# Edge windows of a graph layer: ranges packed into one register each, loops of five tiles, sums on two other engines, x loaded alone

## The reference, cut to what matters

```python
xn = _layernorm(x)
hp = xn @ weight
agg = segment_sum(hp[src] * edge_weight[:, None], dst)      # relu'd later
x = x + relu(agg) + mix(xn)                                 # linear attention
```

## Time and profile before

| | |
|---|---|
| median of three runs | 1304.54 us (1303.4 to 1308.75) |
| the profiled execution's own time | 1310.6 us |
| its span from first to last instruction | 1309.1 us |
| mean granted TensorE clock | 0.929 |
| PE busy | 1117.8 us (85%) |
| DVE busy | 540.6 us (41%) |
| ACT, POOL busy | 347.6 and 83.4 us |
| the windows | from 53.4 to 183.5 us of the span |

### The profile page before, as it was taken

How to read it: one execution, slowest core, us unless ns; L and a number is a source line. 1 busy time by engine, 2 the same in 40 slices (tenths; PEclk the granted TensorE clock), 3 DMA queues, 4 the chain that set the end, 5 groups by cost and what they waited for, 6 DMA issues and landing times.

```text
span 1309.1 us, 19993 instructions
## 1 busy us (share of the span) xinstructions
PE 1117.8 (85%) x7185; PEld 757.1 (58%) x7186; DVE 540.6 (41%) x1434; ACT 347.6 (27%) x881; POOL 83.4 (6%) x130
## 2 busy tenths in 40 slices
PE   2766679988999863999998659998979998988896
PEld 1456564465877651555554347777557777565652
DVE  7565565343555431111111035444325544376430
ACT  1000012012555430222222125554115555011320
POOL 5100000000000032001000050000000000000000
PEclk9897789998999975999999969999989999998898
DMA  7500004010100046940199671000111000000000
GB/s 198 141 1 1 1 1 193 32 57 17 31 26 3 1 185 244 388 177 19 60 401 398 244 271 43 25 9 2 64 73 41 25 9 2 33 1 0 1 1 39
DMA packets 18415, 113.06 MB, mean 86 GB/s; under 512 B 4718, under 2 KB 6245, under 8 KB 14135
## 3 DMA queue, kind: packets, MB, share of 16 engines
q1 hardware_dynamic: 12718, 100.95, 20.3%
q0 software_dynamic: 5632, 11.23, 3.3%
HBM read 103.04 MB, written 9.11 MB: 86 GB/s over the span
## 4 chain that ended last, share of the span: by engine, by line
PE 74%; DVE 8%; DMA 7%; issue 4%; ACT 3%; DVEq 3%; POOL 1%; SPq 0%; POOLq 0%; ACTq 0%
PE psum L514 11%; PE psum L669 8%; PE psum L819 7%; PE psum L800 7%; PE psum L692 5%; PE psum L526 5%; PE psum L723 5%; PE psum L674 4%; PE psum L705 4%; PE psum L581 4%; PE psum L878 3%; PE psum L900 3%; DMA arena<-in_moe_b 2%; PE psum L502 1%; DVE arena L1183 1%
## 5 line engine op out<-in xcount | busy, mean ns | idle before, releaser
L514 PE MATMUL psum<-arena 128*125 128x512 f32 x320 | 142.2, 605 | 2.6 <-ACT arena L913 2.0
L581 PE MATMUL psum<-arena 125*128 x975 | 85.6, 260 | 44.5 <-DVE arena L1183 41.4
L971 ACT ACTIVATE arena<-arena,small 125x625 f32<-125x625 f32 x120 | 97.0, 809 | 90.5 <-DVE small L1312 90.5
L669 PE MATMUL psum<-arena 128*128 128x313 f32 (+1 forms) x384 | 112.2, 443 | 8.5 <-DMA arena<-in_att 7.2
L800 PE MATMUL psum<-arena 128*64 128x512 f32 x448 | 101.7, 607 | 7.4 <-DMA arena<-in_moeW 6.0
L514 PEld LDWEIGHTS psum<-arena 128*125 128x125 f32 x320 | 60.9, 192 | 80.7 <-issue 74.9
L581 PEld LDWEIGHTS psum<-arena 125*128 125x128 bf16 x975 | 74.2, 119 | 54.5 <-issue 52.2
L819 PE MATMUL psum<-arena 128*64 128x256 f32 x896 | 99.8, 381 | 3.7 <-DMA arena<-in_moe_b 3.7
L1029 ACT ACTIVATE arena<-psum,cols 128x64 f32<-128x64 f32 x224 | 47.3, 361 | 198.6 <-PE psum L806 198.6
L669 PEld LDWEIGHTS psum<-arena 128*128 128x128 f32 x384 | 72.2, 194 | 37.9 <-issue 9.7
L1183 DVE TENSOR_SCALAR arena<-arena 125x628 bf16<-125x628 f16 x195 | 66.9, 382 | 63.3 <-issue 28.0
(11 more groups left out here) (242 smaller groups left out, 1335.6 us busy)
## 6 DMA issues: line engine op xcount, KB each, us to landing
arena<-in_moeW SPq DMA_DIRECT2D x16, 4096.0 KB, 17.7
arena<-in_att SPq DMA_DIRECT2D x36, 256.0 KB, 2.8
arena<-in_l1W SPq DMA_DIRECT2D x2, 2048.0 KB, 15.7
rows<-in_rows SPq DMA_DIRECT2D x1, 2500.0 KB
token_rows<-arena POOLq DMA_DIRECT2D x19, 128.0 KB, 10.5
expert_rows<-arena POOLq DMA_DIRECT2D x17, 128.0 KB, 10.0
arena<-token_rows POOLq DMA_DIRECT2D x16, 128.0 KB, 8.3
arena<-in_gnnWo SPq DMA_DIRECT2D x2, 1024.0 KB, 6.2
```

What stands on the lines that cost most here:

```text
L514: mm = pe.matmul(bank(b, NP, D), srcT[:, k, c * NP:(c + 1) * NP], ring[n % 2][:, k, :], start=(k == 0), stop=(k == KC - 1))
L581: mm = pe.matmul(psum[:, o + c * P:o + (c + 1) * P], one_src[:, s, c * NP:c * NP + P], hot_dst[:, bass.ds(e * P, P)], start=False, stop=False,
L669: mm = pe.matmul(bank(b, P, width), aw[:, w, k, :], srcT[:, k, o:o + width], start=(k == 0), stop=(k == KC - 1))
L971: act.activation(Sx[u % 3][h], Sx[u % 3][h], ACT.Exp, bias=small[0:NP, 80 + n:81 + n], scale=-1.0, accum_out=small[0:NP, 120 + n:121 + n]) ...
```

## The change

A round does five tiles, and there are five `one_src` buffers. The first tile and the number of rounds are packed as `64 * first + rounds`, so PE spreads one value instead of three; PE and DVE load one register for each window, all twenty ahead of the first window, and unpack them in registers at each window; the rounds before a window are added up in a register. ACT copies the counts and also the three weight parts (125 x 480) to one of two SBUF buffers; POOL adds the three parts in two instructions. PE waits for ACT's copies instead of DVE's sum. The statistics of x are taken piece by piece as x lands, ahead of `bounds`; the destination one-hot is written behind the layer norm. x is loaded in five pieces, alone; `gnnW` is issued when x is there, `mixWq` and the rest when `gnnW` is there, and POOL's zero rows wait for `gnnW` too. PE waits for the ranges only behind `hp`.

```diff
-GT = 3
+GT = 5
+KG = -(-ET // GT)
...
+        def tile_range(eng, packed):
+            return (eng.snap(packed >> 6, min_val=0, max_val=ET - 1), eng.snap(packed & 63, min_val=1, max_val=KG))
...
-            sp.dma_start(xres[:], ins["x"]).then_inc(ld_x, 16)
+            for c in range(NC):
+                sp.dma_start(xres[:, c, :], ins["x"][:, c, :]).then_inc(ld_x[c], 16)
+            for c in range(NC):
+                sp.wait_ge(ld_x[c], 16)
             sp.dma_start(ring[0], ins["gnnW"]).then_inc(ld_ring[0], 16)
+            sp.wait_ge(ld_ring[0], 16)
             sp.dma_start(ring[1], ins["mixWq"]).then_inc(ld_ring[1], 16)
             sp.dma_start(cols[:], ins["cols"]).then_inc(ld_const, 16)
-            sp.wait_ge(ld_x, 16)
...
-            pool.wait_ge(ld_x, 16)
+            pool.wait_ge(ld_ring[0], 16)
...
-            pool.wait_ge(win_full, NW)
+            for w in range(NW):
+                pool.wait_ge(parts_out, w + 1)
+                n = min(DW, N - DW * w)
+                p3 = parts[w % 2].rearrange("p c (v d) -> p c v d", v=3)
+                pool.tensor_tensor(p3[:, :, 0, 0:n], p3[:, :, 0, 0:n], p3[:, :, 1, 0:n], ALU.add).then_inc(part_sum, 1)
+                pool.wait_ge(part_sum, w + 1)
+                pool.tensor_tensor(WT[:, :, DW * w:DW * w + n], p3[:, :, 0, 0:n], p3[:, :, 2, 0:n],
+                                   ALU.add).then_inc(wt_out, 1)
...
-            for v, spread in enumerate((ident, ident, upper)):
-                mm = pe.matmul(bank(5, 1, WMIN, WMIN * v), w_cols[:, min(v, 1):min(v, 1) + 1], spread[0:NW, 0:WMIN],
-                               start=True, stop=True)
-            mm.then_inc(range_rows, 1)
-            pe.wait_ge(range_ready, 1)
+            pe.matmul(bank(5, 1, WMIN), w_cols[:, 1:2], ident[0:NW, 0:WMIN],
+                      start=True, stop=True).then_inc(range_rows, 1)
...
+            pe.wait_ge(range_ready, 1)
+            ranges = [pe.value_load(bounds[0:1, w:w + 1], min_val=1, max_val=64 * ET + KG) for w in range(NW)]
+            before = 0
...
-            ahead = tile_range(0)
             for w in range(NW):
-                first, k, before = ahead
+                first, k = tile_range(pe, ranges[w])
                 o = window_banks(w)
                 if w >= 4:
-                    pe.wait_ge(wt_out, w - 3)
+                    pe.wait_ge(parts_out, w - 3)
...
-                if w + 1 < NW:
-                    ahead = tile_range(w + 1)
...
+                before = pe.snap(before + k, min_val=w + 1, max_val=(w + 1) * KG)
...
             product_cols("mq", T1, 1, window_out)
+            pe.wait_ge(cnt_out, NW)
...
+            pe.wait_ge(wt_out, NW)
...
+                sums = psum[0:NP, o:o + NC * P].rearrange("p (c x) -> p c x", x=P)
+                act.activation(cntT[:, :, DW * w:DW * w + n], sums[:, :, 3 * DW:3 * DW + n], ACT.Copy).then_inc(cnt_out, 1)
+                if w >= 2:
+                    act.wait_ge(wt_out, w - 1)
+                act.activation(parts[w % 2], sums[:, :, 0:3 * DW], ACT.Copy).then_inc(parts_out, 1)
...
-            ve.tensor_copy(w_cols[:, 1:2], n_i[:, 1:2]).then_inc(range_cols, 1)
+            ve.scalar_tensor_tensor(w_cols[:, 1:2], w_cols[:, 0:1], 64.0, n_i[:, 1:2], ALU.mult,
+                                    ALU.add).then_inc(range_cols, 1)
+            for c in range(NC):
+                ve.wait_ge(ld_x[c], 16)
+                i_ = chunk_stats(xres, c)
+            link(i_)
             ve.wait_ge(range_rows, 1)
-            ve.tensor_copy(bounds, bank(5, 1, 3 * WMIN).rearrange("p (v w) -> p v w", v=3)).then_inc(range_ready, 1)
-            ve.wait_ge(ld_x, 16)
-            layer_norm(0, xres, N1)
+            ve.tensor_copy(bounds, bank(5, 1, WMIN)).then_inc(range_ready, 1)
+            layer_norm(0, xres, N1, stats=False)
+            ve.tensor_tensor(hot_dst4[:, :, 3, :], low.unsqueeze(2).to_broadcast([NP, TP, DW]),
+                             iota_dst.unsqueeze(1).to_broadcast([NP, TP, DW]), ALU.is_equal).then_inc(dst_one, 1)
...
             ve.wait_ge(range_ready, 1)
-            ahead = tile_range(0)
+            ranges = [ve.value_load(bounds[0:1, w:w + 1], min_val=1, max_val=64 * ET + KG) for w in range(NW)]
+            before = 0
             for w in range(NW):
-                first, k, before = ahead
-                if w + 1 < NW:
-                    ahead = tile_range(w + 1)
+                first, k = tile_range(ve, ranges[w])
...
-                if w:
-                    window_sums(w - 1)
-            window_sums(NW - 1)
+                before = ve.snap(before + k, min_val=w + 1, max_val=(w + 1) * KG)
```

More of the change, by code:

```diff
@@ L32 @@
 NW = -(-N // DW)
-SW = N + GT
+SW = N + 3
 EX = 8
@@ L177, in build @@
         zero_bf = take(NP, P, dt=BF16)
-        zero_rows_sb = take(TT, D)
+        zero_rows_sb = at(o_D + TP * 2 * DW, TT, D)
         t_lo, t_hi = take(ET // 2, 2), take(ET // 2, 2)
@@ L182, in build @@
         w_end = take(NW, 8)
-        w_cols = take(NW, 3)
+        w_cols = take(NW, 2)
         n_i = take(NW, 2, dt=I32)
-        bounds = take(1, 3, WMIN, dt=I32)
+        bounds = take(1, WMIN, dt=I32)
+        parts = [at(o_T + 2 * KC * N + i * NC * 3 * DW, NP, NC, 3 * DW) for i in range(2)]
+        assert o_D + TP * 2 * DW + D <= AR
         assert oa[0] <= o_cnt
@@ L240, in build @@
         unit_full, freed_a, freed_v = sem("unit_full"), sem("freed_a"), sem("freed_v")
-        ld_edges, ld_x, ld_const = sem("ld_edges"), sem("ld_x"), sem("ld_const")
+        ld_edges, ld_const = sem("ld_edges"), sem("ld_const")
+        ld_x = [sem(f"ld_x{c}") for c in range(NC)]
         ld_ring = [sem(f"ld_ring{i}") for i in range(2)]
@@ L252, in build @@
         hot_ready, hot_free = sem("hot_ready"), sem("hot_free")
-        win_full, wt_out, cnt_out = sem("win_full"), sem("wt_out"), sem("cnt_out")
+        win_full, cnt_out = sem("win_full"), sem("cnt_out")
+        parts_out, part_sum, wt_out = sem("parts_out"), sem("part_sum"), sem("wt_out")
         fm_min, fm_exp = sem("fm_min"), sem("fm_exp")
@@ L588, in _ @@
                 mm.then_inc(win_full, 1)
+                before = pe.snap(before + k, min_val=w + 1, max_val=(w + 1) * KG)
             def window_out(unit):
                 w = NW - 4 + (unit % 8) // 2
-                pe.wait_ge(wt_out, w + 1)
+                pe.wait_ge(parts_out, w + 1)
             product_cols("mq", T1, 1, window_out)
+            pe.wait_ge(cnt_out, NW)
             for c in range(NC):
@@ L931, in _ @@
                 o, n = 512 * (2 * (w % 4)), min(DW, N - DW * w)
-                act.activation(cntT[:, :, DW * w:DW * w + n],
-                               psum[0:NP, o:o + NC * P].rearrange("p (c v d) -> p c v d", v=4, d=DW)[:, :, 3, 0:n],
-                               ACT.Copy).then_inc(cnt_out, 1)
+                sums = psum[0:NP, o:o + NC * P].rearrange("p (c x) -> p c x", x=P)
[3 more added lines that the diff above has]
+                act.activation(parts[w % 2], sums[:, :, 0:3 * DW], ACT.Copy).then_inc(parts_out, 1)
             def feature_exps(units):
@@ L1138, in _ @@
             i_.then_inc(range_in, 1)
-            ve.tensor_tensor(hot_dst4[:, :, 3, :], low.unsqueeze(2).to_broadcast([NP, TP, DW]),
-                             iota_dst.unsqueeze(1).to_broadcast([NP, TP, DW]), ALU.is_equal).then_inc(dst_one, 1)
             ve.wait_ge(range_turned, 1)
```

## The result

The changed kernel takes **1323.5 us** (median of four runs, 1321.4 to 1326.7) where the kernel before takes 1304.0: a ratio of 1.0144, 95% interval 1.0111 to 1.0177. It is slower by 19.5 us where 31 us less were forecast. The profiled execution took 1324.6 us with a span of 1323.0.

What follows compares the result with a forecast made beforehand. It took PE and DVE waiting on each other in rounds, and register loads at borders, as the bound. Rounds 81.4, borders 17.1 and clock 2.0 made 100.5 us for 130.2; with the front, 31 less: 1273.5 us, range 1259 to 1295.

Steps and rivals of the forecast that it cites:

- The rounds: Window loop: 46 rounds of five tiles at 1.77 us, set by PE's sequencer, 81.4 us.
- The borders without the sum: Between windows: register steps replace loads, 0.9 us a border, 17.1 us for 19; bounds 10 and 27.
- Front part: Before the windows: x at 12.5 us, `hp` ending at 40.4, first tile at 52.0 against 53.39.
- The clock: PE in the windows: a low start costs 2.0 us, then the high clock is taken as held.
- The sum: All windows: rounds, borders and clock start, 100.5 us instead of 130.2; with the front, 31 us less.
- POOL against DVE: Windows: POOL's sums hold up DVE's one-hots, 20 x 1.0 us on top, 1282 us; chance 0.17.
- the loads stick out whole: PE's twenty range loads, behind `hp`: no overlap with it, +8.3 us, 1282 us; chance 0.10.
- x alone: Front: x loaded alone is not early, at 18.6 us, moving all by 6, 1280 us; chance 0.06.
- slower: PE's matmuls in the windows: low clock throughout, 140 us against 130 before, 1302 to 1313 us; chance 0.05.

Runs made afterwards that it cites:

- reg_sum: The changed kernel with the rounds before a window held in one register on PE and DVE; 1269.7 us, 0.9727 of the kernel before.
- five_alone: The kernel before with only rounds of five tiles and five one-hot buffers; 1296.7 us, 0.9925 of the kernel before.

## Why the prediction was wrong

**The step that failed** is in the borders: I counted the running sum as one register step at a border, and costed three steps there with 0.36 to 1.26 us. The sum is made inside the rounds, once in each, out of all earlier windows: 564 steps more on each engine, 57.7 us of the windows, instead of 19 steps. I asked what a register step costs and not how many there are and where they stand. My price of a bare step was near enough (0.12 with its gap; measured 0.10). What I took for "a register" in the code was an expression; a value's bounds in the source say nothing of where it is computed. The diff alone did not say so, but a rival with its price should have stood there: everything that the change computes from a loop-carried value, worked out for the case that it is computed where it is used.

**The rest held, point by point.**
- *The rounds.* PE's sequencer as the bound at 1.77 us a round: 1.80 in the first window of the changed kernel, 1.80 and then 1.90 in reg_sum, whose sequencer goes from step to step through a whole round. That 1.77 came out so near is in part luck. The rounds of five_alone, which have the steps that I counted, take 1.66 in the first window; in reg_sum there is a step more in every round and another from the second window on, by all signs the unpacking, which I had put at the borders.
- *The borders without the sum.* Taken at 0.9, measured at some 0.3 in reg_sum, below my lower bound even: a term too dear by 11 us. It has no step of unpacking in it, only those of `reg_add` and of the loop's start. The unpacking stands in the rounds, and the longer rounds behind the first window (1.90) take back five of the 11.
- *Front part.* `hp` to end at 40.4, it was 40.6. x was not there at 12.5 but at 15.9, of which one us was waited for. Before, it came at 19.3; the 18.6 that I took for it is where DVE's wait began. PE's loads were to begin at 32.7 us and did. With 0.65 us for most of them and not 0.88 they ended at 46.6, so the first tile came at 48.2, between the two values I gave: 5.2 us gained instead of 1.3. By the Trainium skill's 64 entries (Advanced Engine Details and Errata, Engine Queue Depths) they would have begun some six us earlier; the measurement (7.9 us, 18 of `hp`'s matmuls) sides with the earlier trace rows. That the loads would then "be done with `hp`" did not follow either: by my 0.88 us each, twenty of them from 26.4 us on end at 44.0 (an estimate from these 64 entries).
- *The clock.* Held from 60 us on wherever the rounds were short, as in reg_sum; in the changed kernel it fell, as a consequence.
- *The sum.* 100.5 us of windows were forecast; with the register they take 93.5, and the time is 1269.7 and 1264.5 us in two groups, where 1273.5 was forecast for this mechanism.
- *POOL against DVE* exists and is small; *the loads stick out whole* did not come; *x alone* was half early (15.9, between 12.5 and 19.3); the *slower* rival had the wrong mechanism: it needed the low clock throughout, which came late and cost little.

Where the expected gain went, by the windows and the first tile: the front gave 5.2 us, five tiles 10.8, one packed load instead of three and then none at borders most of the other 26, where the sums are made nothing that can be measured; the rebuilt sum took 57.7.

## What to carry to other kernels

When a value is carried from one dynamic loop to the next, ask where it is computed, and hold it in a register that is written once a turn; a value written as an expression of others can be evaluated at each use, as the sum was here and, by the counts of steps, the unpacked range. The cost of a sum of all earlier turns then grows with the square of the turns. In the trace this shows as idle time of the engine that ends on nothing ("issue") and grows along the program; count the sequencer's steps of the line. A forecast of a change in control code should price it twice, once for each place where the steps may stand.

## What the runs showed that I had not expected

- A sequencer's register step takes 0.03 to 0.04 us in the profile but one every 0.10 us on PE (30 from 176.6 to 179.6), so a chain of thirty is nearly as long as two rounds of matmuls at the high clock.
- PE's register loads took 0.54 us near 50 us in the kernel before and 0.30 in the changed one from 32.7 to 45.6, while transfers ran in both. What made the difference stays open.
- Two engines that hand each other buffers pass on the slower sequencer's time: with PE cured alone the windows still took 127.8 us.
- One load at a border costs 0.76 us, five buffers notwithstanding. It stands in the sequencers of both engines; that this is why the buffers do not hide it was not tested.
